# Flamingo block on one core: mask and maximum by VectorE instead of mask products on TensorE, and the last attention's keys made ahead of the experts

## What is computed

```
A0  16 heads of 64: scores = q.k/sqrt(64); where(causal | padding, -1e30, scores); softmax; @v
F0  gated bitlinear FFN 128 -> 512 -> 128, activations quantized per row
A1  16 heads of 8: scores = q.k/sqrt(8); where(mask == 0, -1e9, scores); softmax; @v
MOE top 2 of 8 experts with a capacity, gelu, gates
A2  one head of 128, masked by positions
F2  absmean FFN with gelu and layernorm
A3  16 heads of 8, keys from the context ctx, no mask; softmax; @v
F3  squared-relu bitlinear FFN with rmsnorm, activations quantized per row
```

## Time and profile before

| what | value |
|---|---|
| median of 3 runs | 485.50 us |
| span of the profiled execution | 482.6 us |
| median less span (start and end, outside the span) | 2.9 us |
| PE busy | 388.5 us, 81% |
| DVE busy | 287.2 us, 60% |
| ACT busy | 263.1 us, 55% |
| POOL busy | 180.6 us, 37% |
| chain of waits, share of the span | PE 61%, ACT 11%, POOL 9%, DVE 7%, issue 7%, DMA 3% |

### The profile page before, as it was taken

How to read it: one execution, slowest core, us unless ns; L and a number is a source line. 1 busy time by engine, 2 the same in 40 slices (tenths; PEclk the granted TensorE clock), 3 DMA queues, 4 the chain that set the end, 5 groups by cost and what they waited for, 6 DMA issues and landing times.

```text
span 482.6 us, 9945 instructions
## 1 busy us (share of the span) xinstructions
PE 388.5 (81%) x3550; PEld 281.1 (58%) x3564; DVE 287.2 (60%) x859; ACT 263.1 (55%) x781; POOL 180.6 (37%) x294
## 2 busy tenths in 40 slices
PE   3866999999997898999962999427778999889633
PEld 0645777767876665665541899315555666665522
DVE  3151575688687878665562121643546566898884
ACT  3234757676675778877631433422464766555532
POOL 3186334333424311355363000388726442221120
PEclk9597999999999999999985899855699999999955
DMA  8990000000000030000003241111000000000001
GB/s 338 394 381 6 1 2 1 1 2 2 2 1 1 1 133 1 1 13 18 20 22 93 59 130 36 45 33 27 7 0 1 3 1 1 2 2 3 3 0 43
DMA packets 7135, 22.11 MB, mean 46 GB/s; under 512 B 1215, under 2 KB 3503, under 8 KB 6575
## 3 DMA queue, kind: packets, MB, share of 16 engines
q1 hardware_dynamic: 6063, 19.38, 11.1%
q0 software_dynamic: 1024, 2.10, 1.5%
HBM read 14.60 MB, written 6.88 MB: 44 GB/s over the span
## 4 chain that ended last, share of the span: by engine, by line
PE 61%; ACT 11%; POOL 9%; DVE 7%; issue 7%; DMA 3%; SPq 0%; POOLq 0%; another core or an unknown queue 0%; DVEq 0%; ACTq 0%
PE bank L839 6%; PE bank L908 6%; PE bank L866 5%; ACT prob L565 5%; PE bank L1031 4%; PE bank L1022 3%; POOL moe_rows L488 3%; PE bank L822 3%; PE bank L854 3%; PE bank L903 3%; PE bank L917 3%; PE bank L810 3%; DVE mx L1236 3%; PE bank L888 2%; PE bank L975 2%
## 5 line engine op out<-in xcount | busy, mean ns | idle before, releaser
L565 ACT ACTIVATE prob<-bank,mx 128x128 f32<-128x128 f32 x256 | 82.3, 384 | 23.4 <-DVE mx L1236 23.2
L1236 DVE TENSOR_REDUCE mx<-bank 128x4 f32<-128x512 f32 x96 | 63.9, 682 | 41.0 <-PE bank L839 21.5
L468 POOL TENSOR_TENSOR prob<-prob,rden 128x512 f32<-128x512 f32 x32 | 33.2, 1039 | 69.2 <-DVE rden L1258 69.2
L550 ACT ACTIVATE probT<-bank 128x512 f32<-128x512 f32 x64 | 39.5, 617 | 29.9 <-PE bank L866 29.8
L866 PE MATMUL bank<-pack,prob 128*128 128x128 f32 x256 | 41.5, 286 | 7.6 <-POOL prob L468 4.6
L443 POOL TENSOR_TENSOR rstd<-rstd,minus_half 128x1 f32<-128x1 f32 x72 | 41.3, 573 | 6.0
L441 POOL TENSOR_SCALAR rstd<-mv 128x1 f32<-128x1 f32 x64 | 12.4, 193 | 83.0 <-DVE mv L1211 79.6
L866 PEld LDWEIGHTS bank<-pack,prob 128*128 128x128 f32 x256 | 28.7, 143 | 16.4 <-POOL prob L468 6.6
L488 POOL DMA_INDIRECT moe_rows<-yrows_d,row_of x16 | 16.0, 999 | 52.2 <-DMA yrows_d<-o_n 48.3
L462 POOL TENSOR_SCALAR xn<-pack,mv,rstd 128x128 f32<-128x128 f32 x32 | 25.9, 811 | 5.9 <-POOL rstd L443 5.4
L565 ACT ACTIVATION_READ_ACCUMULATOR prob<-bank,mx 128x1 f32 x128 | 27.9, 218 | 0.0
(11 more groups left out here) (233 smaller groups left out, 965.2 us busy)
## 6 DMA issues: line engine op xcount, KB each, us to landing
yrows_d<-moe_rows SPq DMA_DIRECT2D x2, 1510.0 KB, 21.2
pack<-pack_d SPq DMA_DIRECT2D x1, 2112.0 KB, 15.7
expert<-experts_d SPq DMA_DIRECT2D x4, 514.0 KB, 8.5
pack<-experts_d SPq DMA_DIRECT2D x4, 514.0 KB, 5.1
pack<-pack_d SPq DMA_DIRECT2D x1, 2048.0 KB, 10.3
xrows_d<-moe_rows SPq DMA_DIRECT2D x1, 1080.0 KB, 21.0
moe_rows<-xrows_d SPq DMA_DIRECT2D x8, 135.0 KB, 3.0
yrows_d<-o_n SPq DMA_DIRECT2D x8, 135.0 KB, 1.8
```

What stands on the lines that cost most here:

```text
L468: pool.tensor_tensor(part, part, r.to_broadcast([P, GH, P]), ALU.mult).then_inc(E[A0]["norm"].sem, 1)
L550: act.activation(dst, src, ACT.Identity if kw else ACT.Copy, **kw).then_inc(E[layer][name].sem, 1)
L565: act.activation(prob[:, g % 2, P * j:P * j + P], bank[S_BANK[g % 2]][:, P * j:P * j + P], ACT.Exp, bias=mx[:, g % 2, j:j + 1], **kw).then ...
L1236: dve.tensor_reduce(out, bank[S_BANK[g % 2]][:, :].rearrange("p (h t) -> p h t", h=GH), AX.X, ALU.max, negate=True).then_inc(E[layer]["max ...
```

## The change

**Mask and maximum.** `mask_scores` and its 64 products are gone, and the scores are written to the bank alone. On DVE `masked_top` takes the place of `top_of` in A0 and A1: for each head of a group one `tensor_tensor_reduce` of 128x128 that reads the scores in PSUM and the mask in SBUF, adds them, negates, writes the result back to PSUM over the scores, and puts the minimum into the head's bias. `exps` reads with a scale of -1 and waits for all four heads of its group.

```
-            def mask_scores(it, layer, g):
-                claim(it, layer, f"s{g}")
...
-                pe.matmul(bank[S_BANK[g % 2]][:, :].rearrange("p (h t) -> p h t", h=GH), identb[:, :],
-                          (neg0 if layer == A0 else neg1)[:, bass.ds(it.b, 1), :].to_broadcast([P, GH, P]), start=True, stop=False)
...
             def scores0(it, c):
                 for a in range(2):
-                    mask_scores(it, A0, 2 * c + a)
+                    claim(it, A0, f"s{2 * c + a}")
...
-                                        start=False, stop=(i == GH - 1))
+                                        start=True, stop=True)
...
+            def masked_top(it, layer, g):
+
+                wait(dve, layer, "scores", it, g + 1)
...
+                for j in range(GH):
+                    s = bank[S_BANK[g % 2]][:, P * j:P * j + P]
+                    dve.tensor_tensor_reduce(s, s, (neg0 if layer == A0 else neg1)[:, it.b, :], -1.0, 3e38, ALU.add, ALU.min,
+                                             mx[:, g % 2, j:j + 1]).then_inc(E[layer]["max"].sem, 1)
...
             def exps(it, layer, g):
-                wait(act, layer, "max", it, g + 1)
+                wait(act, layer, "max", it, GH * g + GH)
...
-                                   bias=mx[:, g % 2, j:j + 1], **kw).then_inc(E[layer]["probs"].sem, 1)
+                                   bias=mx[:, g % 2, j:j + 1], scale=-1.0, **kw).then_inc(E[layer]["probs"].sem, 1)
```

```
+                    (keys3, (None, None, None, None, None, None, None, 253.042)),
+                    (fold, (None, None, None, None, None, None, None, 253.142))],
...
-            walk(dve, PLAN, stages, before={(A0, 3): means, (MOE, 0): weigh_experts, (A2, 0): start_last, (F3, 0): squared_bias})
+            walk(stages, [(61.1, means), (257, weigh_experts), (259, keys3_sb), (258.9, fold), (384, squared_bias)])
...
-        expert = [expert2[:, n, :] for n in range(2)] + [packed[1][:, EXPERT * n:EXPERT * n + EXPERT] for n in range(EXPERT_BUFS - 2)]
+        expert = [expert2[:, n, :] for n in range(2)] + [packed[3][:, EXPERT * n:EXPERT * n + EXPERT] for n in range(EXPERT_BUFS - 2)]
...
-            wait(sp, A0, "y", Item(B - 1, B - 1))
+            sp.wait_ge(tern_dve, 3 * len(TERNARY))
```

More of the change, by code:

```diff
@@ L74, in at @@
         return self.per * item.b + (self.base + (self.per if j is None else j))
[L77 to L141, removed]
@@ new lines, in walk @@
+def walk(stages, once=(), run=lambda layer, fn, it, *args: fn(it, *args)):
+    queue = []
+    for layer, entries in stages.items():
+        for b in range(B):
+            for fn, *args, places in entries:
+                if places[b] is not None:
+                    queue.append((places[b], len(queue), run, (layer, fn, Item(b, b), *args)))
+    for at, fn in once:
+        queue.append((at, len(queue), fn, ()))
+    while queue:
+        at, n, begin, args = head = min(queue, key=lambda entry: entry[0:2])
+        queue.remove(head)
+        rest = begin(*args)
+        if rest is not None:
+            if next(rest, stages) is not stages:
+                queue.append((at + TURN, n, lambda rest=rest: rest, ()))
@@ L349, in build @@
             emptied[MOE, f"h{t}"] = ("gelu", t + 1)
+        E[A0]["mean"] = Event(wsum_dve, 0, len(TERNARY))
+        emptied[A0, "w"] = ("mean", 1)
+        E[ROUTE]["keys_a"], E[ROUTE]["keys_d"] = Event(k4_act, 0, 3 * GH - 1), Event(k4_dve, 0, 3 * GH - 1)
+        emptied[ROUTE, "k0"], emptied[ROUTE, "k1"] = ("keys_a", 1), ("keys_d", 1)
+        E[ROUTE]["folded"] = Event(fold_dve, 0, FT + 1)
+        emptied[ROUTE, "fold"] = ("folded", 1)
         def wait(eng, layer, name, item, j=None):
@@ L533, in _ @@
                 A3: [
[L534 to L537, removed]
+                    (rs, A3, (362.459, 367.214, 375.614, 385.498, 396.431, 407.91, 419.423, 429.543))],
                 F3: [
[L539 to L544, removed]
+                    (rs, F3, (398.391, 409.997, 421.323, 431.444, 439.827, 450.218, 458.877, 466.23)),
@@ L674, in k4_sb @@
                 act.wait_ge(k4_pe, 2 * n + c + 1)
+                if n:
+                    wait(act, A1, "scores", Item(B - 1, B - 1))
+                    wait(act, A0, "y", Item(B - 1, B - 1))
                 for into, at in ((kt[0], 0), (kt[1], GH)) if n else ((kz4, 0),):
@@ L742, in _ @@
             prepare()
-            walk(act, PLAN, stages, before={(MOE, 0): route_exp, (A2, 0): lambda: k4_sb(1, 0)})
+            walk(stages, [(257.2, route_exp), (257.7, keys3_sb)])
         @block.tensor
@@ L1080, in places, with fold @@
                 pe.matmul(out, onesb[:, :], before_b[:, it.b, :], start=False, stop=True).then_inc(E[ROUTE]["places"].sem, 1)
-            def fold():
+            def fold(it):
                 pe.wait_ge(tern_dve, 3 * len(TERNARY))
-                wait(pe, ROUTE, "row", Item(B - 1, B - 1))
+                claim(it, ROUTE, "fold")
                 for t in range(FT):
@@ L1208, in ln_stats @@
                     wait(dve, BEFORE[layer], "resid", it)
+                wait(dve, layer, "rs", it.back(2))
                 do = chain(layer, "ln", it)
@@ L1313, in hid0 @@
                 wait(dve, F0, "up", it)
+                wait(dve, F0, "hid", it, 1)
                 do = chain(F0, "hid", it, 1)
@@ L1370, in hid2_stats @@
                 wait(dve, F2, "gelu", it)
+                wait(dve, F2, "rs_hid", it.back(2))
                 do = chain(F2, "hid", it)
@@ L1529, in k4_sb @@
                     dve.wait_ge(prep_dve, 3)
+                    wait(dve, A1, "scores", Item(B - 1, B - 1))
+                    wait(dve, A0, "y", Item(B - 1, B - 1))
                 for into, at in ((kt[0], 0), (kt[1], GH)) if n else ((kz4, 0),):
```

416 lines of the change are left out of this document (227 added, 189 removed).

## The result

The changed kernel takes **508.96 us** (median of four runs, 507.23 to 511.03) against 485.46 for the kernel before, a ratio of 1.0497 (95% interval 1.0463 to 1.0531). The forecast was 495.5, the range 483 to 508: the direction was right, the size was less than half of the truth, and the time lies just outside the range.

The account below looks back on a forecast made before the run. The prediction took PE, busy 81% of the span, as nearly full, with DVE deciding in F0 with A1. Its terms, 0.15 + 3.9 + 1.0 + 4.0 + 1.0 = +10.05 on 485.5, gave 495.5 us, range 483 to 508.

Parts of the forecast that it names:

- Price of a masked maximum: On DVE in A0 and A1: 0.275 us a head, 1.1 a group, +0.5 against 0.60 for one packed reduction.
- A0 without F0: Three periods of A0: PE saves four products, 1.06 us, against +0.5 on the chain; -0.55 each, -1.7 in all.
- The order on DVE: DVE's instruction order: no term of its own; only the delays from moved hid0 and hq3 chains were priced.
- `hid0`: hid0 wholly ahead of the first maximum: +0.3 a period in A0 with F0, +0.3 at A0's end.
- F0 with A1: DVE decides here: four groups at +0.5, less its 0.71 wait, give +1.3 a period; three periods, +3.9.
- A3 with F3: Fourth maximum behind hq3 and the residual: PE waits 0.45 a period, +1.8, less 0.8 in the tail; +1.0.
- A1 with ROUTE: Four periods and the tail: two groups at 0.5 against 0.8 of PE's saving, +0.2 each, +1.0.
- Keys ahead of the experts: Keys, fold and copies before the first expert delay it by +4.0; behind the last expert the gain is 0.
- Rival 3: Before the first expert: the keys are hidden, so the +4.0 goes; 491.5 us; chance 0.12.
- The dear pair: Masked maxima on DVE: a head takes 0.37, a group +0.9, DVE becomes the bound; +12, 507.5 us; chance 0.20.
- The rival that the maxima fit beside PE: PE stays the bound and maxima fit beside its work: 473.5 us, or 482 with half the saving; chance 0.18.

Follow-up runs that it names:

- pe_mask: The changed kernel with the mask products back on PE and one reduction per group on DVE; keys ahead and new DVE order kept: 505.35 us.
- order_only: The kernel before with DVE's new order alone, mask products on PE and keys behind the last expert: 502.19 us.
- mask_only: The kernel before with the masked maxima alone, DVE's order and the keys' place as before: 488.01 us.
- u_quant: The changed kernel with DVE's old order only where F0's first item comes in (quant0 taking turns with A0's item 3): 503.41 us.
- u_hid: The changed kernel with DVE's old order only in the stretch of all eight hid0: 502.25 us.
- u_last: The changed kernel with DVE's old order only from F2 to the end: 505.59 us.
- old_order: The changed kernel, masked maxima and keys ahead kept, with DVE's instructions in the order of the kernel before: 491.62 us.
- even_groups: The kernel before, with the masked maximum on DVE only for the first group of each pair of groups: 490.82 us.
- odd_groups: The kernel before, with the masked maximum on DVE only for the second group of each pair of groups: 481.03 us.
- odd_not7: The kernel before with masked maxima on DVE for each pair's second group, except in A0's last item, which keeps its products on PE: 480.24 us.

## Why the prediction was wrong, by its steps

- **Price of a masked maximum, 0.275 a head:** right, 0.25. The Trainium skill ("VectorE: DVE Perf Modes", sections "The TRN2 errata" and "Two Vector instructions with no wait between them") led to an estimate of 1.28 us for a group; the trace has 1.0, so the measurement decides on the size, while the rule's direction (one large instruction is better than four small ones) and the two instructions per head are borne out.
- **A0 without F0, -1.7:** -1.84 in the trace, but that the saved products did it is not shown: `pe_mask`, which has the products, stands at -1.53 at the same row and `order_only` at -0.74, while `mask_only` without products gains only 0.50. That the size fits is luck as far as these runs tell.
- **The order on DVE: this is the step that failed.** The prediction followed two chains that moved, `hid0` and `hq3`, and the part on the change says that DVE's order differs in three places. It differs in many more, since every chain comes back 0.203 places behind its last instruction and so mostly runs to its end ahead of anything placed later. The one that mattered most, `quant0` of item 0 ahead of the maxima of A0's item 3, has no term in the sum at all: 5.8 us by the rows, 4.4 to 5.55 by the times of `u_quant`. No row had to be measured to see it; it stood in the order, and the trace of before shows that the chain's third instruction waited for POOL.
- **`hid0`, +0.3 a period in A0, +0.3 at its end and no term of its own in F0 with A1:** mis-sized, 5.6 by the rows, 5.5 to 6.7 by the times (`u_hid`). In A0 with F0 it was near (1.5 over three periods). At A0's end it is 2.35, and the masked maxima take 1.6 more (`mask_only`), 3.9 together where the prediction had 0.75: it counted the maximum's delay only, but PE waited 4.73 us and then ran at half clock.
- **A3 with F3, +1.0:** mis-sized, 5.5 by the traces; the times of `u_last` give 3.4 with a wide spread. The prediction let the transposed maximum wait 0.45 a period, +1.8; that wait grew by 1.2. What it lacked is the residual, for which PE waits 4.0 in the stage: it counted the residual as work ahead of the maximum and not as a thing that PE needs.
- **F0 with A1, +3.9:** 2.75 in the trace, and the mechanism is not the one forecast. The masked maxima alone lose 1.1 there (`mask_only`), where four groups at +0.5 less a wait of 0.71 were to give 1.3 a period; the other 1.75 are `hid0`'s place (`u_hid`), which had no term. That the sum comes near is luck.
- **A1 with ROUTE, +1.0:** 3.3 in the trace, mis-sized. The old order loses nearly the same there, timeline of `old_order` at the rows of 142.47, 195.29, 242.09 and 307.87:

```profile
140.63 1.04 POOL L606 TENSOR_TENSOR prob<-prob,rden 128x512 f32<-128x512 f32 x1 [0.67 <-DVE rden L1418]
...
196.00 0.19 POOL L579 TENSOR_SCALAR rstd<-mv 128x1 f32<-128x1 f32 x1 [0.31 <-DVE mv L1362]
...
245.66 0.18 POOL L579 TENSOR_SCALAR rstd<-mv 128x1 f32<-128x1 f32 x1 [2.25 <-DVE mv L1362]
...
315.14 0.99 POOL L626 DMA_INDIRECT moe_rows<-yrows_d,row_of  x1 [52.31 <-DMA yrows_d<-o_n]
```

  These are -1.84, +0.71, +3.57 and +7.27: A0 keeps its gain, A1 with ROUTE loses 2.9 with the old order too, the keys take 3.7. So this loss is the maxima's own, and it is the first group's: 4.7 in `even_groups`, a gain of 0.9 in `odd_groups`. Two first groups an item start their exponentials 0.41 us later; how the loss divides between that and saved products that were only waiting time is not shown.
- **Keys ahead of the experts, +4.0, gain 0:** right in mechanism and size, 3.6 in the trace, 2.5 to 3.6 by the runs. Rival 3, the keys hidden, is out with it.
- **The rivals.** The dear pair gave 507.5, close to the measured time, by a mechanism that is refuted, which is luck: the pair is cheap. The rival that the maxima fit beside PE is true of the second group of each pair alone, and that half is worth 3.2 us (`odd_groups`) to 4.8 (`odd_not7`).

## What to carry to other kernels

When an order comes from a table of times, compare the whole list on the engine, and for each chain that now runs through ask what its instructions wait for and who stands behind: one chain with a wait for another engine, ahead of work that was ready, cost 4 to 6 us here, more than the masked maxima with their eight instructions a group (3.1). Before moving work from a full engine to one with room, look at which of its places lie on the chain between engines: the same instruction put the exponentials 0.4 us later in the first group of a pair and not at all in the second, and moving only that second half beat both kernels. Work put into another engine's idle gap must be summed to its end with the clock of that gap, and what waits behind it is the price.

## What the runs showed of the hardware that was not expected

- A wait of TensorE costs more than its length where its clock falls: after 4.63 us of idle time the granted clock was 0.50, and eight matmuls took 2.08 us instead of 1.16. The place where one chain stood cost 5.8 us by the rows, where PE's wait grew by 4.2 (from 0.39 to 4.63).
- Whether the clock falls is not settled by the length of the wait: at A0's end two waits of 0.71 and 1.49 us left it at 1.00 in one kernel and were followed by 0.65 in another.
- The read-out behind a masked maximum is 0.14 us long by its record, but a head starts every 0.25 us against 0.20 for a plain instruction of this size: by estimate 0.05 us for each read-out.
